# Moving Wg's load, weight splits, adds and gathers between queues in the first three slots of a cross-attention and permuted-FFN kernel

## The reference

```
def _L0_xattn_ref(inp_q, inp_k, inp_v, Wt, Wp, Wg, Wz, gn_w, gn_b):
    t = einsum('oc,bcd->bod', Wt, inp_v)
    p = einsum('oc,bcd->bod', Wp, inp_q)
    g = einsum('oc,bcd->bod', Wg, inp_k)
    ...
    att = sum(pg * gg, axis=-1, keepdims=True)        # per batch and group of 64 channels
    y = einsum('goi,bgid->bgod', Wzg, att * tg)
    ...
    yn = (yg - mu) * rsqrt(var + EPS)                 # over a group
    return yn * gn_w[None, :, None] + gn_b[None, :, None] + residual
x = x + _L0_xattn_ref(_layernorm(x), ctx, ctx, Wt, Wp, Wg, Wz, gn_w, gn_b)
t = _layernorm(x)[:, perm]          # per head h of 128 features
t = gelu(einsum('bhd,hdm->bhm', t, up))
t = einsum('bhm,hmd->bhd', t, down)
x = x + t[:, unperm]
```

## Time and profile before

| | |
|---|---|
| median of 3 runs | 1555.33 us (1555.02 to 1556.88) |
| the profiled execution's own time | 1552.91 us |
| its span, first to last instruction | 1551.1 us |
| TensorE busy | 1506.6 us, 97% |
| VectorE busy | 1183.7 us, 76% |
| ScalarE busy | 1067.0 us, 69% |
| GpSimd busy | 985.2 us, 64% |
| mean granted TensorE clock | 0.991 |

### The profile page before, as it was taken

The page is one execution under the profiler, slowest core; times in us unless marked ns, Lnnn a source line. Parts: engine busy times, 40 slices in busy tenths (PEclk is TensorE's granted clock), DMA queues, the critical chain, the costliest instruction groups (busy, mean ns, idle before and its releaser), DMA issues.

```text
span 1551.1 us, 19543 instructions
## 1 busy us (share of the span) xinstructions
PE 1506.6 (97%) x6592; PEld 1236.4 (80%) x6592; DVE 1183.7 (76%) x1498; ACT 1067.0 (69%) x1321; POOL 985.2 (64%) x781
## 2 busy tenths in 40 slices
PE   8999889997999999999999999999999999999998
PEld 6877767886888888888888888888888888877876
DVE  5768857875788767887778876788778887889776
ACT  4634827672786848876588756878468774899876
POOL 1596657267792638817487266852578345898886
PEclk9999999998999999999999999999999999999999
DMA  9789868877486755778467783677847677758886
GB/s 326 260 307 359 278 202 298 300 223 260 157 281 245 236 172 183 277 257 245 140 199 272 267 270 117 219 248 257 263 132 263 237 250 216 231 195 260 276 279 211
DMA packets 166871, 374.79 MB, mean 242 GB/s; under 512 B 14964, under 2 KB 80500, under 8 KB 158580
## 3 DMA queue, kind: packets, MB, share of 16 engines
q1 hardware_dynamic: 141424, 281.25, 55.2%
q0 software_dynamic: 25344, 92.29, 16.8%
HBM read 287.45 MB, written 86.03 MB: 241 GB/s over the span
## 4 chain that ended last, share of the span: by engine, by line
PE 74%; POOL 9%; DVE 6%; DMA 4%; ACT 4%; issue 3%; POOLq 0%; SPq 0%; ACTq 0%; DVEq 0%
PE PP L863 19%; PE PP L877 17%; PE PP L931 16%; PE PP L916 16%; PE PP L890 5%; DVE R L1058 2%; POOL X L1296 2%; POOL FB L1304 1%; POOL FB L1307 1%; POOL out L1312 1%; DMA WW<-w_scratch 1%; ACT Z L1005 1%; POOL FB L1289 1%; ACT PP L1020 1%; DVE R L1217 1%
## 5 line engine op out<-in xcount | busy, mean ns | idle before, releaser
L916 PE MATMUL PP<-GG,WW 128*128 128x512 f32 x1536 | 391.2, 391 | 12.4 <-DVE GG L1212 10.8
L863 PE MATMUL PP<-R 128*128 128x512 f32 x1536 | 357.5, 393 | 13.7 <-DVE R L1058 12.6
L877 PE MATMUL PP<-R,WC 128*128 128x512 f32 x1536 | 351.3, 390 | 2.6 <-ACT Z L972 2.6
L863 PEld LDWEIGHTS PP<-R 128*128 128x128 f32 x1536 | 290.5, 190 | 76.0 <-issue 10.7
L916 PEld LDWEIGHTS PP<-GG,WW 128*128 128x128 f32 x1536 | 288.0, 188 | 76.6 <-issue 16.8
L877 PEld LDWEIGHTS PP<-R,WC 128*128 128x128 f32 x1536 | 289.4, 188 | 63.2 <-ACT Z L972 3.0
L1296 POOL TENSOR_TENSOR X<-X,RAW 128x512 f32<-128x512 f32 x128 | 211.8, 1687 | 115.1 <-DVE bn L1043 79.0
L931 PE MATMUL PP<-R,WW 128*128 128x512 f32 x1050 | 269.3, 392 | 4.2 <-DVE R L1217 2.6
L1020 ACT ACTIVATE PP<-PP 128x1024 f32<-128x1024 f32 x256 | 261.8, 1023 | 0.0
L1217 DVE TENSOR_TENSOR R<-PP,R 128x1024 fp32r<-128x1024 f32 x175 | 213.5, 1220 | 60.7 <-ACT PP L1020 60.5
L1019 ACT ACTIVATE R<-PP 128x1024 fp32r<-128x1024 f32 x175 | 180.0, 1029 | 100.5 <-PE PP L916 100.3
(11 more groups left out here) (95 smaller groups left out, 1612.2 us busy)
## 6 DMA issues: line engine op xcount, KB each, us to landing
WW<-w_scratch SPq DMA_DIRECT2D x152, 512.0 KB, 5.1
X<-in_x SPq DMA_DIRECT2D x32, 1024.0 KB, 5.4
RAW<-in_cx SPq DMA_DIRECT2D x32, 1024.0 KB, 7.4
RAW<-in_xT SPq DMA_DIRECT2D x63, 512.0 KB, 5.7
RAW<-in_cT SPq DMA_DIRECT2D x63, 512.0 KB, 6.9
xg_scratch<-FB SPq DMA_DIRECT2D x104, 256.0 KB, 4.7
w_scratch<-WW POOLq DMA_DIRECT2D x16, 1024.0 KB, 7.1
HX<-wp_scratch SPq DMA_DIRECT2D x7, 1024.0 KB, 8.2
```

What stands on the lines that cost most here:

```text
L863: t = eng.matmul(s_bank(c1), l[:, part(c1)], r, start=(dt == 0 and j == 0), stop=(dt == ND - 1 and j == 2))
L877: t = eng.matmul(PP[2 + ot // 2][:, ot % 2, :], WC[:, l, ct, part(ot)], u[:, r + ct, :], start=(ct == 0 and j == 0), stop=(ct == NT - 1 an ...
L916: t = eng.matmul(PP[slot["up", f, p]][:, e, :], wt[:, l, part(2 * p + e)], g[:, r, :], start=(j == 0), stop=(j == 2))
```

## The change

- Heads 10 to 15 and 0 to 3: `w_hi` goes to ScalarE; all ten use FB0 to FB3 (heads 2 and 3 had FB4 and FB5), and the times of load, split and store are closer together and earlier.
- Batch 0's sixteen `add_c` go to VectorE. `root_x` of batch 0 comes later in GpSimd's queue.
- `load_wg` of slots one and two is put behind `load_wpl` and the last `store_x`.
- The three first `load_s` of slot two come earlier.
- The first three gathers of slots zero to two have times of their own, ahead of the last split in slot two.

```diff
--- before.py
+++ after.py
@@ -410,11 +410,11 @@
         for i in YHEADS:
             if h in YHEADS[i]:
                 return [("raw", slot["c", i, 1 + YHEADS[i].index(h) // 2])]
-        k = 4 if h in (2, 3) else 2 * (h % 2)
+        k = 2 * (h % 2)
         return [("FB", k), ("FB", k + 1)]
 
     def load_raw(h):
-        sem = f"rh{h}" if h in YHEADS[1] + YHEADS[2] else f"rw{2 if h in (2, 3) else h % 2}"
+        sem = f"rh{h}" if h in YHEADS[1] + YHEADS[2] else f"rw{h % 2}"
         free["rw", h] = take(*raw_w(h))
         n.dma("rw", h, sem=sem, count=2)
         slot["rw", h] = raw_w(h)[0], sem
@@ -567,11 +567,11 @@
         put(10.5 + 0.1 * pr, fold_hi, pr)
         put(10.7 + 0.1 * pr, fold_lo, pr)
     for k, h in enumerate((10, 11, 12, 13, 14, 15, 0, 1, 2, 3)):
-        t = 20 + 2.2 * k + (1.4 if k > 5 else 0) if k < 8 else 4.5 * k + 2.5
+        t = 17 + 1.8 * k
         put(t, load_raw, h)
-        put(t + 4, w_hi, h)
-        put(t + 4.1, w_lo, h)
-        put(t + 4.2, keep_w, h)
+        put(t + 3.3, w_hi, h)
+        put(t + 3.4, w_lo, h)
+        put(t + 3.5, keep_w, h)
 
     base = [0, 36, 88] + [88 + 68 * k for k in range(1, B - 2)]
     f = 0
@@ -589,7 +589,7 @@
             put(y0 + 8.1 + 1.8 * k + late, w_lo, h)
             put(y0 + 8.2 + 1.8 * k + late, keep_w, h)
         for j in range(8):
-            put(s0 + (S_LOAD[j] if i > 1 else (-14, -10, -8)[j] if i and j < 3 else 2 * j - (5 if i or j else 10)), load_s, i, j)
+            put(s0 + ((-18.5, -17.5, -13)[j] if i == 2 and j < 3 else S_LOAD[j] if i > 1 else (-14, -10, -8)[j] if i and j < 3 else 2 * j - (5 if i or j else 10)), load_s, i, j)
         for dt in range(ND):
             t = s0 + (dt - 2.6 if i < 2 else S_FIRST[i > 2][dt] if dt < 4 else S_LATE.get(dt, dt - 2.6))
             put(t, s_hi, i, dt)
@@ -605,10 +605,10 @@
             for ct in range(NT):
                 put(5.4 + 1.7 * ct, load_x, i, ct)
         put(y0 + 2.2 + late, aggr_x, i)
-        put(y0 + 2.3 + late, root_x, i)
+        put(y0 + (2.3 + late if i else 8), root_x, i)
         for q, t in enumerate((s0 + 9, s0 + 11, s0 + 13, y0 + 1.5 + late)):
             put(t, load_c, i, q)
-        put(y0 + (9.4 if 0 < i < 3 else 4.2), load_wg, i)
+        put(y0 + (12.4 if 0 < i < 3 else 4.2), load_wg, i)
         for q, t in enumerate((y0 - 3, y0 + 0.4, y0 + 4.3, y0 + 8.3)):
             put(t, y_hi, i, q)
             put(t + 0.2, y_lo, i, q)
@@ -679,7 +679,7 @@
         end = len(gs)
         for g, (b, h, x) in enumerate(gs):
             lead = f0 + 2 * g
-            put(max(lead - 6.5, v0 - 4 + 0.1 * g if i < 3 else v0 - 3 if g == 0 else v0 - 1), gather, f, b, h)
+            put(v0 - 3.6 + 0.1 * g if i < 3 and g < 3 else max(lead - 6.5, v0 - 3 if g == 0 else v0 - 1), gather, f, b, h)
             put(lead - (2.45 if g else 3.0), g_hi, f, b)
             put(lead - (2.1 if g else 2.8), g_lo, f, b)
             put(lead - 2.05, resid, f, b)
@@ -939,6 +939,12 @@
                 pr = a[0]
                 act.wait_ge(*at["wc", pr])
                 eng.copy(WC[:, 0, 2 * pr:2 * pr + 2, :], PP[2 + pr][:]).then_inc(S["wch"], 1)
+            elif stage == "w_hi" and a[0] not in YHEADS[1] + YHEADS[2]:
+                h = a[0]
+                act.wait_ge(*at["rw", h])
+                for t in free["wsp", h]:
+                    act.wait_ge(*t)
+                eng.copy(WW[h % 2][:, 0:4:2, :], raw_tile(h)).then_inc(S["whi"], 1)
             elif stage == "wp_hi":
                 act.wait_ge(*at["wp",])
                 eng.copy(HX[:], RAW[slot["wp"]][:]).then_inc(S["wph"], 1)
@@ -1063,6 +1069,12 @@
                 u = R[slot["y", i, q]]
                 eng.tensor_tensor(u[:, 4:8, :], RAW[slot["c", i, q]][:], f32(u[:, 0:4, :]),
                                   ALU.subtract).then_inc(S["ylo"], 1)
+            elif stage == "add_c" and a[0] == 0:
+                i, q, ct = a
+                dve.wait_ge(*at["c", i, q])
+                dve.wait_ge(*at["x", i, ct])
+                eng.tensor_tensor(X[:, ct, cols(q)], X[:, ct, cols(q)], RAW[slot["c", i, q]][:, ct, :],
+                                  ALU.add).then_inc(S["xc"], 1)
             elif stage == "sum_c":
                 i = a[0]
                 dve.wait_ge(*at["cs", i, NQ - 1, NT - 1])
@@ -1236,7 +1248,7 @@
                 eng.dma_start(raw_tile(h)[:, 0, :], up[h]).then_inc(S[slot["rw", h][1]], 16)
                 eng.dma_start(raw_tile(h)[:, 1, :].rearrange("p (t d) -> p t d", t=NM),
                               down[h].rearrange("(t p) d -> p t d", p=P)).then_inc(S[slot["rw", h][1]], 16)
-            elif stage == "w_hi":
+            elif stage == "w_hi" and a[0] in YHEADS[1] + YHEADS[2]:
                 h = a[0]
                 pool.wait_ge(*at["rw", h])
                 for t in free["wsp", h]:
@@ -1288,7 +1300,7 @@
                 pool.wait_ge(*at["perm",])
                 eng.indirect_dma_start(out=FB[:, f % NFB, :], out_offset=None, in_=xg_d[b][:, :],
                                        in_offset=perm_of(h)).then_inc(S[f"fb{f % NFB}"], 16)
-            elif stage == "add_c":
+            elif stage == "add_c" and a[0]:
                 i, q, ct = a
                 pool.wait_ge(*at["c", i, q])
                 pool.wait_ge(*at["x", i, ct])
```

## The result

The changed kernel takes 1549.05 us in the median (1546.82 to 1551.73, 6 runs) beside 1555.5 us (1553.89 to 1556.88, 6 runs): the ratio is 0.996, with a 95% interval of 0.9947 to 0.9973. It is faster by 6.4 us, and was forecast to be faster by 15.1; the range ended at 1549. The profiled execution took 1551.73 us around a span of 1549.9 us. So the two traces differ by only 1.2 us in span, and milestones read from them show some 5 us less than the measured gain. What they show well is where single waits went.

What follows compares the result with a forecast made beforehand. The prediction took TensorE, busy 1506.6 of 1551.1 us, as the bound, its idle time and lowered clock as the prize. Terms 0 - 7.6 - 1 - 6.5 = -15.1 took 1555.3 to 1540 us, range 1531 to 1549.

Steps and rivals of the forecast that it cites:

- B: Slot one, Wg behind Wp's low half: wait for `wp_scratch` and its half clock go, -7.6 us, ends -8.4 and -3.
- D: Slot two, gathers ahead of head 7's split: wait of 2.5 in place of 8.0, -6.5 us, ends -10 and -4.
- Rival 4: Slot one: Wp's low half held by something else, or gather takes over the wait; B is 0, 1548 us, chance 0.07.
- C: Slot two's S tiles issued some 20 us sooner, away from the weight loads: -1 us, ends -1.5 and +1.
- A: Opening of slot one, 5.2 us late behind ScalarE's casts, given back later: taken as 0, ends -6 and +8.
- rival 1: A dear opening: rounds of 13 us make slot one open 11 late, 5 given back; +7, 1547 us, chance 0.2.
- rival 2: The whole give-back: VectorE collisions and full DMA stretch were all the S stage's loss; A is -6, 1534 us, chance 0.17.
- rival 3: Ring through ScalarE: rounds of 15.4 us, slot one opens 20.8 late, 5 given back; +15.8, 1556 us, chance 0.06.
- The adds: Sixteen adds moved to VectorE, some 10.4 us of work within 27 us idle in slices two and three: cost nothing.

Runs made afterwards that it cites:

- weights part alone: Kernel before with ten casts on ScalarE, four buffers, closer times, batch 0's adds on VectorE and the later root: 1559.15 us, ratio 1.0016.
- experiment three: Kernel before with both queue edits, Wg last and slot two's first three gathers ahead of the last split: 1548.29 us, ratio 0.9941.
- experiment one: Kernel before with one edit, Wg behind Wp's low half and the last store of x in slots one and two: 1547.1 us, ratio 0.9933.
- the slower ring: Experiment six: the change with its heads 2.3 apart in place of 1.8 and the cast 4.3 behind the load in place of 3.3: 1543.4 us, ratio 0.9919.
- experiment seven: Kernel before with casts on ScalarE in four buffers, adds on VectorE and later root, at pitch 2.3 and split delay 4.3: 1553.43 us, ratio 0.9974.
- nine: The slower ring with batch 0's sixteen adds back on GpSimd and the root at its old place: 1545.48 us, ratio 0.9926.
- experiment ten: The change with slot two's S tiles loaded where they were before: 1549.48 us, ratio 0.9953.

## Why the prediction was wrong

The direction was right; the size was not. Forecast 0 - 7.6 - 1 - 6.5; measured, by the ratios: weights part alone +2.5, Wg alone -10.4, gathers alone -4.5, and the S tiles, taken out of the change, 0. Together they would be -12.4, but Wg and gathers overlap: as a pair they give -9.2 (experiment three), and -9.2 + 2.5 = -6.7 is the measured -6.4 within the noise. Two steps failed: the gather's landing in B, and D's gather, which had another condition and was counted in full beside B.

**B, Wg behind Wp's low half.** Right in its mechanism: no wait for `wp_scratch`, V's clock whole. Alone it paid its term or more (10.4, its interval 7.5 to 13); slot two's wait shrank as well. Rival 4, that it would not be realised, is out for Wg alone. In the change its second half, that the gather takes over the wait, came close: 4.52 + 2.7 = 7.2 us stand in slot one where 5.86 + 2.55 = 8.4 stood, and of all the times named rival 4's 1548 is the nearest. The mis-sized term is "perhaps 0.8 us of wait remains". By the numbers beside it none remains (214 + 3.6 + 1.6 = 219.2, wanted at 220.9), so 0.8 was an allowance. It rests on "the gathered tile is there 3.6 us later", a landing read where little else was in flight. It measured 9.7 us in the change, 7.3 in experiment one, 9.4 in the slower ring. The wait was 4.52 us with 2.7 us of clock behind it, in place of 0.8. The early start of V uncovers the gather: before, V itself was late and at half clock, and the gather hid beneath it.

**D, the gathers ahead of head 7.** The step "now the gather goes at 371.73 + 0.56" left out the other condition of the gather, that the last store of x has left its buffer. It waited 2.99 us for it alone and 6.30 in the change, and landed in 6.1 us rather than 3.6. The remaining wait was 6.22 us, not 2.5. And the term was counted in full beside B, although Wg's place shortens the same wait to 4.88. Terms that end at one wait were added as if each had its own.

**C, slot two's S tiles.** A gain of 1 us, ends -1.5 and +1: taking it out of the change moved the ratio by 0.0007, out of the slower ring by 0.0027, neither clear of the noise. What it takes from the weights' waits it adds to the gather's.

**A, the opening.** The term was 0 and measured +2.5, inside its ends (-6 and +8), and that is luck: two errors nearly cancel. The opening was 13.7 us late by the earlier trace rows's 114.30 against 127.96, where I had 5.2 (rival 1 had 11). These are ScalarE's casts of heads 10 and 2:

```profile
71.21 1.04 ACT L947 CAST WW<-FB 128x1024 fp32r<-128x1024 f32 x1
...
122.59 1.05 ACT L947 CAST WW<-FB 128x1024 fp32r<-128x1024 f32 x1 [2.59 <-DMA FB<-in_down]
```

Four rounds took 51.4 us, 12.8 each, which is rival 1's 13. The round was counted at 11.5 us "as the rounds at 80 to 110 lie in the quiet", which holds for the kernel before, but the slot one S tiles go out in the same stretch, and `in_down` took 10.2. Slot zero had a wait of 5.50 us at an eviction, which I had "within this number". Against that, V began 2.2 us after 212.7: 11.5 us were given back, where I had 5. That is rival 2's half of the story. The pieces of x1 stand beside no split now:

```profile
141.21 1.28 DVE L1186 SCALAR_TENSOR_TENSOR Z<-Z,sm,X 128x1024 f32<-128x1024 f32 x1
143.98 2.47 DVE L1186 SCALAR_TENSOR_TENSOR Z<-Z,sm,X 128x1024 f32<-128x1024 f32 x2
```

1.28 us each, where the earlier trace rows show up to 3.42. The S and Y stages run with no wait at all. The rule of the Trainium skill that I had weighed ("GPSIMD Engine Reference", Specifications: GpSimd shares SBUF interfaces with VectorE) agrees with these rows.

**The ring through ScalarE, rival 3,** was the right place at the wrong size. A cast that waits for its load holds evictions; it cost slot zero a wait of 5.50 us, and the slower ring takes it away. Undone in that way, A becomes -4.0 (experiment seven) and the whole -12.6. By my estimate the forecast of 15 would have needed a gather that lands in the quiet as well (the slower ring still waits 5.88 and 4.84 us for it); no run shows that.

**The adds.** "Cost nothing" held: nine against six shows no difference.

## What to carry to other kernels

A wait removed ahead of a short stage uncovers the next transfer, and that transfer then flies beside those that were moved behind the wait: take its landing from rows where as much is in flight, not from the quiet. When two edits shorten the chain to the same product, count the later of the two chains once. In a queue in which nothing passes, put a step that waits for a load behind whatever TensorE wants; half a unit more from head to head and one more from load to cast were worth as much as the whole edit. And before a milestone of one trace is laid to an edit, look at the waits ahead of the edit's place: one of them moved by 3 us between kernels that are the same up to there.

## What the runs showed of the hardware

The indirect gather of 128 rows of 2 KB landed in 3.7 us when little was in flight (228 GB/s in its window), in 6.5 beside Wg, head 9's store and a load of 0.5 MB (403 GB/s in 213 to 217 us of experiment one), and in 9.6 with S tiles of the next slot as well. It is GpSimd's, the S tiles are SP's, and without them alone it takes 7.5 (experiment ten): the queue that issues it gives no shelter. The Trainium skill says so ("DMA: Bandwidth & Descriptors", Issuing engines are not separate DMA queues), and these rows agree. Nearly a factor of two showed on ordinary loads: `in_down`, 256 KB, 5.3 us in the change's 100 to 112 us and 9.7 in its 90 to 100. I had expected such landings only near 117 us.
